# Causal attention: score maxima and chunk sums turned by DMA as 16-bit values, GpSimd's splitting given out in pieces

## What is computed

```python
q = _apply_rope(q, cos, sin)
k = _apply_rope(k, cos, sin)
groups = NH // NKV
k = jnp.repeat(k, groups, axis=2)
v = jnp.repeat(v, groups, axis=2)
scale = HD ** (-0.5)
scores = jnp.einsum('bqhd,bkhd->bhqk', q, k) * scale
causal = jnp.tril(jnp.ones((S, S), dtype=bool))
scores = jnp.where(causal[None, None], scores, jnp.finfo(scores.dtype).min)
probs = jax.nn.softmax(scores, axis=-1)
attn = jnp.einsum('bhqk,bkhd->bqhd', probs, v).reshape(B, S, NH * HD)
```

## Time and profile before

| | us |
|---|---|
| median of 3 runs (1744.45 to 1746.79) | 1745.84 |
| the profiled execution, whole | 1756.45 |
| the profiled execution, span of the trace | 1754.1 |

### The profile page before, as it was taken

How to read it: one execution, slowest core, us unless ns; L and a number is a source line. 1 busy time by engine, 2 the same in 40 slices (tenths; PEclk the granted TensorE clock), 3 DMA queues, 4 the chain that set the end, 5 groups by cost and what they waited for, 6 DMA issues and landing times. The chain is left out here.

```text
span 1754.1 us, 29582 instructions
## 1 busy us (share of the span) xinstructions
PE 1631.0 (93%) x9040; PEld 804.0 (46%) x9040; DVE 1172.6 (67%) x3195; ACT 947.3 (54%) x2069; POOL 553.5 (32%) x842
## 2 busy tenths in 40 slices
PE   7799998899999999999999999998885799999996
PEld 3367655333333333333333333332774355555554
DVE  6632788799888888888888888860765243434342
ACT  6043554166667667676777767767654233333332
POOL 3441338073505003030030300000376244444443
PEclk9899998699999999999999999999986899999999
DMA  5000000321030300303003030000457577777775
GB/s 162 1 7 19 1 2 7 61 42 22 2 61 2 62 2 1 62 2 61 2 2 62 2 61 2 2 1 7 138 193 271 116 130 130 129 130 129 131 125 72
DMA packets 252194, 105.76 MB, mean 60 GB/s; under 512 B 208064, under 2 KB 247880, under 8 KB 252040
## 3 DMA queue, kind: packets, MB, share of 16 engines
q1 hardware_dynamic: 233296, 80.62, 21.6%
q0 software_dynamic: 13392, 18.49, 6.2%
q10 hardware_dynamic: 5352, 4.76, 0.8%
HBM read 30.88 MB, written 23.67 MB: 31 GB/s over the span
## 5 line engine op out<-in xcount | busy, mean ns | idle before, releaser
L1675 ACT ACTIVATE prob<-pS 128x512 f32<-128x512 f32 (+3 forms) x1280 | 597.1, 534 | 256.3 <-PE pS L1563 133.9
L1732 DVE TENSOR_REDUCE mx<-pM 128x1 f32<-128x512 f32 x768 | 503.0, 685 | 70.3 <-PE pM L1543 66.5
L1543 PE MATMUL pM<-KT,QT 96*128 96x512 bf16 (+3 forms) x1280 | 443.6, 356 | 8.7 <-DMA QT<-Qt 4.7
L1559 PE MATMUL pS<-QT,KT 99*128 99x512 bf16 (+3 forms) x1280 | 416.2, 350 | 3.7 <-ACT prob L1675 2.9
L1578 PE MATMUL pO<-prob,VV 128*32 128x512 f32 (+3 forms) x2560 | 299.9, 540 | 14.6 <-ACT prob L1675 14.3
L1728 DVE CUSTOM_DVE_ANT_0 junk<-pM,mask_row 128x128 bf16<-128x128 f32 (+3 forms) x512 | 241.5, 484 | 46.2 <-PE pM L1543 42.9
L2413 PE MATMUL pH<-w13T,QKV 128*128 x568 | 256.8, 595 | 15.4 <-ACT QKV L2439 15.4
L1543 PEld LDWEIGHTS pM<-KT,QT 96*128 96x128 bf16 x1280 | 124.0, 98 | 268.5 <-DVE mx L1732 110.0
L1468 POOL CAST mpart<-mneg 128x16 bf16<-128x16 f32 x32 | 6.8, 211 | 663.2 <-DVE mneg L1740 663.2
L2472 DVE TENSOR_TENSOR QKV<-QKV,pH 128x512 f32<-128x512 f32 x71 | 48.8, 688 | 233.7 <-issue 199.8
L1559 PEld LDWEIGHTS pS<-QT,KT 99*128 99x128 bf16 x1280 | 123.4, 98 | 143.2 <-ACT prob L1675 79.6
(11 more groups left out here) (356 smaller groups left out, 1954.2 us busy)
## 6 DMA issues: line engine op xcount, KB each, us to landing
raw<-in_ffn_w_dram SPq DMA_DIRECT2D x48, 256.0 KB
QKV<-queue SPq DMA_DIRECT2D x71, 136.0 KB, 2.6
out_dram<-x ACTq DMA_DIRECT2D x8, 512.0 KB
x<-_attn_hidden_states_dram SPq DMA_DIRECT2D x14, 256.0 KB, 5.4
QKV<-QKV SPq DMA_TRANSPOSE x142, 2.5
QT<-mrow SPq DMA_DIRECT2D x128, 3.0 KB
out_dram<-QKV POOLq DMA_INDIRECT x71, 3.9
wc_s<-in_attn_Wc_dram SPq DMA_DIRECT2D x1, 1024.0 KB, 8.2
```

The costliest lines, as they stand in the source:

```text
L1543: last = nc.tensor.matmul(pM[:, bank, 0:w], QT[0:ROWS, par, h, qt * P:(qt + 1) * P], KT[0:ROWS, par, 512 * part:512 * part + w], start=Tru ...
L1559: last = nc.tensor.matmul(pS[:, p % NSC, lo:512], KT[0:ROWS + 3, par, kt * P:(kt + 1) * P], QT[0:ROWS + 3, par, h, 512 * c + lo:512 * c + ...
L1675: nc.scalar.activation(prob[:, n % 3, h, lo:512], pS[:, p % NSC, lo:512], ACT.Exp, scale=SCALE).then_inc(s.head_exp, 1)
L1732: nc.vector.reduce_max(mx[:, h, qt, part:part + 1], pM[:, plan.bank[item], 0:w], AX.X).then_inc(s.unit_max, 1)
```

## The change

M leaves PE and ACT. `maxima_parts` writes the parts into columns 0 to 11 of a tile of 4 x 128 columns, the rest of which is zero. SP turns that tile by one DMA transpose (512 columns), waits until it has landed, and then issues the same four DMAs as before (`rows_in`). SP does so in the plan's place of M among its other work.

O leaves PE for every chunk but the last. POOL copies `oS` as 16-bit values, low and high halves apart, into `oh` (`attended_parts`, 1024 values in each partition). SP turns `oh` by one DMA transpose of 1024 columns into `ohT` (`attended_turned`), behind `rows_in` and `turned_in` of that step where there are any. Three steps after that POOL copies the halves together into `oC` (`attended_joined`, 1024 values), and six steps after it DVE divides and stores from `oC` (`chunk_put`). DVE's next `chunk` waits for POOL's copy of the chunk before, not for PE's transposes.

The banks `pM` are handed round among the units alone, and the last O. POOL's queue is now built by step: in each step the maxima's parts, the copies of a chunk's sums, and then at most one piece of other work; `prepare` is cut into six pieces (the keys, and five of the queries). `split` is the same work, in two helpers.

```diff
-        for n, item in enumerate(order):
-            by = {"M": "mrow_out", "U": "unit_max", "O": "o_put"}[item[0]]
+        for n, item in enumerate(x for x in order if x[0] == "U" or x == ("O", CH * NG - 1)):
+            by = {"U": "unit_max", "O": "o_put"}[item[0]]
...
+                def rows_in(k):
+                    par, cols = (k // CH) % 2, slice(512 * (k % CH), 512 * (k % CH) + 512)
+                    sp.wait_ge(s.mparts, k + 1)
+                    if k:
+                        sp.wait_ge(mrow_in[(k - 1) % 2], 64 * ((k - 1) // 2) + 64)
+                    sp.dma_start_transpose(mrow[:, :, :], mpart[:, :, :].rearrange("p j n -> p (j n)")).then_inc(mrow_out[k % 2], 16)
+                    sp.wait_ge(mrow_out[k % 2], 16 * (k // 2) + 16)
+                    for h in range(GRP):
+                        sp.dma_start(QT[ROWS:ROWS + 3, par, h, cols],
+                                     mrow[3 * h:3 * h + 3].rearrange("p j n -> p (j n)")).then_inc(mrow_in[k % 2], 16)
+
+                def attended_turned(k):
+                    sp.wait_ge(s.o_parts, k + 1)
+                    if k:
+                        sp.wait_ge(s.o_join, k)
+                    sp.dma_start_transpose(ohT[:, :, :], oh[:, :]).then_inc(o_in[k % 2], 16)
                 turned_in(0)
-                for k in range(CH * NG):
-                    par, cols = (k // CH) % 2, slice(512 * (k % CH), 512 * (k % CH) + 512)
-                    sp.wait_ge(s.mrow_out, k + 1)
-                    if k >= 2:
-                        sp.wait_ge(mrow_in[k % 2], 64 * (k // 2))
-                    for h in range(GRP):
-                        sp.dma_start(QT[ROWS:ROWS + 3, par, h, cols], mrow[3 * h:3 * h + 3, cols]).then_inc(mrow_in[k % 2], 16)
-                    if k % CH == 2 and k // CH + 1 < NG:
-                        turned_in(k // CH + 1)
+                for x in plan.before:
+                    if x[0] == "M":
+                        rows_in(x[1])
+                for n in range(len(STEPS)):
+                    for x in plan.beside[n]:
+                        if x[0] == "M":
+                            rows_in(x[1])
+                            if x[1] % CH == 2 and x[1] // CH + 1 < NG:
+                                turned_in(x[1] // CH + 1)
+                    for k in contexts(n):
+                        attended_turned(k)
...
+                def attended_parts(k):
+                    pool.wait_ge(s.o_out, k + 1)
+                    if k:
+                        wait_apart(pool, o_in[(k - 1) % 2], 16 * ((k - 1) // 2) + 16)
+                    nc.gpsimd.tensor_copy(oh[:, :].rearrange("p (a n) -> p a n", a=2), apart(oS)).then_inc(s.o_parts, 1)
+
+                def attended_joined(k):
+                    wait_apart(pool, o_in[k % 2], 16 * (k // 2) + 16)
+                    if k:
+                        pool.wait_ge(s.o_put, k)
+                    nc.gpsimd.tensor_copy(apart(oC), ohT[:, :, :].rearrange("p (a j) n -> p a (j n)", a=2)).then_inc(s.o_join, 1)
                 values_in(0)
+                todo = []
+                for n in range(-1, len(STEPS)):
+                    for x in plan.before if n < 0 else plan.beside[n]:
+                        if x in plan.last_unit:
+                            k = plan.last_unit[x]
+                            maxima_parts(k)
+                            first, last = after(k)
+                            todo = first + todo + last
+                    for k in contexts(n):
+                        attended_parts(k)
+                    for k in contexts(n - 3):
+                        attended_joined(k)
+                    if todo:
+                        work(todo.pop(0))
...
-                    for k in contexts(n):
-                        chunk_out(k)
                 values(last_step)
                 chunk_out(CH * NG - 1)
...
                 def chunk(k, n):
                     dve.wait_ge(s.pv, n)
                     if k:
-                        dve.wait_ge(s.o_mm, k)
+                        dve.wait_ge(s.o_parts, k)
                     nc.vector.tensor_copy(oS[:, :], pO[:, :]).then_inc(s.o_out, 1)
...
-                    dve.wait_ge(s.o_mm, k + 1)
-                    o = pM[:, plan.bank[("O", k)], :].rearrange("p (k h d) -> p k h d", k=4, h=GRP)
+                    if k == LAST:
+                        dve.wait_ge(s.o_mm, 1)
+                    else:
+                        dve.wait_ge(s.o_join, k + 1)
+                    o = (pM[:, plan.bank[("O", k)], :] if k == LAST else oC[:, :]).rearrange("p (k h d) -> p k h d", k=4, h=GRP)
...
                 for n, (gi, c, kt) in enumerate(STEPS):
                     for x in plan.beside[n]:
                         beside(x)
-                    for k in contexts(n):
+                    for k in contexts(n - PUT_LATER):
                         chunk_put(k)
                     if n and kt == 0:
                         chunk(CH * gi + c - 1, n)
```

More of the change, by code:

```diff
@@ L1216, in schedule @@
     return before, beside
+LAST = CH * NG - 1
+PUT_LATER = 6
 def contexts(s):
@@ L1248, in __init__ @@
         for k in range(CH * NG):
-            self.units_through[k] = max(self.count[x] for x in order if x[0] == "U" and CH * x[1] + x[3] // 4 == k)
-        self.last_unit = {x: CH * x[1] + x[3] // 4 for x in order
+            self.units_through[k] = max(self.count[x] for x in self.count if x[0] == "U" and CH * x[1] + x[3] // 4 == k)
+        self.last_unit = {x: CH * x[1] + x[3] // 4 for x in self.count
                           if x[0] == "U" and self.count[x] == self.units_through[CH * x[1] + x[3] // 4]}
@@ L1307, in stage6 @@
         f = Names({n: sem("q_" + n) for n in fnames})
+        o_in = [sem(f"c_o_in{n}") for n in range(2)]
+        mrow_out = [sem(f"c_mrow_out{n}") for n in range(2)]
         mrow_in = [sem(f"c_mrow_in{n}") for n in range(2)]
@@ new lines, in after, with work @@
+                def after(k):
+                    gi = k // CH + 1
+                    first = [("keys", gi)] + [("queries", gi, n) for n in range(5)] if k % CH == 1 and gi < NG else []
+                    last = [("norm",)] if k == 2 else []
+                    if k % CH == 3 and gi < NG:
+                        last.append(("values", gi))
+                    return first, last + [("turn", TB + 2 * (k - 1) + n) for n in range(2) if 1 <= k <= TB // 2]
+                def work(item):
+                    if item[0] == "keys":
+                        if item[1] == NKV:
+                            pool.wait_ge(f.turned_pool, NPOOL + TB)
+                        if item[1] == 1:
+                            pool.wait_ge(f.first_ready, 3)
+                        prepare_keys(item[1])
+                    elif item[0] == "queries":
+                        prepare_queries(item[1], item[2])
+                    elif item[0] == "norm":
+                        residual_norm()
+                    elif item[0] == "values":
+                        values_in(item[1])
+                    else:
+                        turn(item[1])
@@ L1494, in _ @@
+                assert not todo
+                for n in range(len(STEPS) - 3, len(STEPS)):
+                    for k in contexts(n):
+                        attended_joined(k)
             @block.tensor
@@ L1664, in _ @@
                         projected_pair(item[1])
-                    else:
-                        beside(item)
                 def exponential(n, h):
@@ L1680, in _ @@
                 for n in range(len(STEPS)):
-                    extra = plan.beside[n]
-                    for place, head in enumerate((0, 1, None, 2, 3)):
-                        for x in extra[place * len(extra) // 5:(place + 1) * len(extra) // 5]:
-                            beside(x)
-                        if n + 1 < len(STEPS) and head is not None:
-                            exponential(n + 1, head)
+                    if n + 1 < len(STEPS):
+                        for h in range(GRP):
+                            exponential(n + 1, h)
             @block.vector
@@ L1770, in _ @@
                         chunk(CH * gi + c - 1, n)
-                chunk(CH * NG - 1, len(STEPS))
-                chunk_put(CH * NG - 1)
+                for n in range(len(STEPS) - PUT_LATER, len(STEPS)):
+                    for k in contexts(n):
+                        chunk_put(k)
+                chunk(LAST, len(STEPS))
+                chunk_put(LAST)
 CAP = B * L + P
```

108 lines of the change are left out of this document (47 added, 61 removed).

## The result

| | before | after |
|---|---|---|
| median, us | 1745.84 (1744.45 to 1746.79) | 1759.62 (1757.58 to 1762.43) |
| ratio, with its 95% interval | | 1.0075 [1.0061, 1.0089] |
| span of the profiled execution, us | 1754.1 | 1760.7 |
| first to last step of the stage, us | 862.3 | 876.9 |

The changed kernel is slower by 13.8 us. The forecast was 5.1 us faster, with a range up to 1757. The last row of the table is the distance from the first value product of the stage to that of its last step, worked out from the trace. The stage alone is 14.6 us longer, which is all of the loss. (The profiled execution of before was itself 10.6 us above its median, so the two spans aren't to be compared.

A forecast was written before the change was run, and what follows sets the result against it. PE was taken to bound the attention's long stretch (420 to 1180 us), DVE's order the chunk ends. Terms: -23.5 - 0.5 + 1.5 + 17.4 = -5.1 us off the 1745.8 median, so 1740.7 us, range 1723 to 1757.

The forecast's parts named there:

- The stall: Place 12, groups 1 to 6: DVE's division waits for late sums, delaying PE's value product; 2.9 us each, 17.4 us lost.
- the prediction's other price: For `turned_in`: at a documented 261 GB/s a wide transpose takes 2.0 us, and DVE waits 0.3 us instead of 2.3.
- Rival 2: POOL's copies of the chunk sums take 2.4 us, so each group loses 5.3 us; 1755.1 us, slower; chance 0.16.
- nothing else is caught: Behind the waiting division at place 12: banks hold four units, PE's own work until the value product is under 2 us.
- fourth rival: Long stretch: PE's freed time doesn't return, as DVE follows too closely; half of 23.5 us lost, 1752.5 us; chance 0.06.
- The saving: PE's stream: 28 Os at 0.43 us and 28 Ms at 0.41 us spared, 23.5 us, plus 0.5 at the start.
- The Ms: Each spares PE 0.41 us: its own 0.32, and the matmul ahead takes 0.22 instead of 0.31; 28 counted.
- the 0.5 for M 1: At the start, M 1 stands between the last early unit and the first scores, DVE idle; 0.5 us saved, an estimate.
- The last chunk: The DMAs of the maxima's rows are issued from 1180.5 instead of 1179.02 us, 1.5 us lost.
- even with no wait: Place 12: the division, formerly at place 5, costs its 0.63 us there even if it needn't wait for the sums.
- Rival 1: At place 12 the sums are back in time, DVE doesn't wait, a group loses 0.63; -18.7, 1727.1 us; chance 0.24.
- Rival 3: DVE's division product from `oC` contends with POOL, 0.6 us more each, 3.6 ahead of the copy; 1744.3 us; chance 0.10.

The follow-up runs named there:

- fill_12: The changed kernel with twelve score products repeated at place 12 of groups 1 to 6, where PE would stand idle: 1753.27 us, ratio 1.0048.
- m_only: The changed kernel with only the maxima turned by DMA; chunk sums go through PE and are divided at once, as before: 1745.74 us, ratio 0.9993.
- sums_first: The changed kernel with SP turning a chunk's sums ahead of the next group's five wide transposes, not behind them: 1736.70 us, ratio 0.9952.
- prepare_whole: The changed kernel with POOL splitting the queries in one go behind the keys, as before, not a piece per step: 1759.52 us, ratio 1.0081.
- put_later_7: The changed kernel with the division seven steps after the turning of the sums instead of six: 1744.08 us, ratio 0.9987.

## Why the prediction was wrong, step by step

**The stall was forecast nearly to the tenth.** The maxima, SP's queue and the copies in the changed kernel, counted from the maxima of each group, against the prediction's chain (its times minus 801.5):

| event | forecast | measured, groups 1 to 6 |
|---|---|---|
| `turned_in` issued to the end | 22.5 | 21.4 to 23.0 |
| sums of c = 0 joined by POOL | 27.3 | 26.4 to 29.2, mean 27.4 |
| value product of place 12 | 31.3 | 30.5 to 33.3, mean 31.5 |

The stall was 17.4 us by forecast and 18.8 measured, from 2.1 to 4.9 us a group where 2.9 was forecast for each. The five wide transposes took 11.9 to 13.4 us, as in the kernel before (12.0 to 13.3), so the 2 us that wide transposes of 2.0 us each would have saved, by the prediction's other price for them, didn't come. Of its terms: the turning of 1024 columns issues in 1.25 us (1.5 forecast), its own landing is 3.2 us in the median, and POOL's copies take 1.04 us to take the halves apart and 1.33 to join them (1.2 for both). Rival 2, with 2.4 us a copy, is out.

```profile
L1403 SPq DMA_TRANSPOSE ohT<-oh x31: 1232/1253/1761, 369.9 to 1203.3; - x31
...
DMA to landing us min/median/max: 3.0/3.2/4.8
```

```profile
L1558 POOL COPY oC<-ohT x31: 1317/1332/1357, 385.1 to 1206.5; 128x1024 uint16<-128x1024 uint16 x31
```

```profile
L1552 POOL COPY oh<-oS x31: 1035/1040/1042, 368.9 to 1202.2; 128x1024 uint16<-128x1024 uint16 x31
```

**The step that failed is what stands behind the stall.** The prediction said of the waiting division that "nothing else is caught", since "the banks hold four units", and counted a stall of 2.9 us as a loss of 2.9. But PE was caught: it ran out of free banks, and its nine waits for DVE's maxima, 15.4 us, are the sign that the prediction had set for its fourth rival. That alone costs nothing more, since the value product waits for the copy in any case: it comes 31.5 us after the maxima, and 31.3 had been forecast. What the prediction left out is how fast PE works afterwards: it looked only for who is late. It read a granted clock of 1.00 in the earlier trace rows and took it as given, though it forecast six gaps of a kind that this stretch didn't have. Measured: +10.9 us at step 12 in six groups, shown by fill_12 to be the clock (9.1 us of it went in the five groups whose clock stayed at full). With this term alone the forecast would have been -5.1 + 10.9 = +5.8 us. The Trainium skill, page "TensorE: Matmul & The Clock Gate", sections "What's actually happening" and "HAM oscillation — how this bites in real kernels", says that TensorE's clock is throttled to half unless the engine's activity releases it, and that waits of TensorE in the middle of a kernel can bring the half clock back each time. The trace agrees (granted 0.50 behind a gap of 2.89 us), though not every wait did it: the one of 2.34 us in the kernel before left the clock at 1.00. It is a rule that spoke against this change, and the prediction hadn't weighed it.

**The saving was 19.8 us and not 24.0.** The price of an O is right: -0.44 at each of the places 0, 4, 12 and 24, 0.43 forecast. But the first group's Os, which the prediction put at nothing, gave it too, so the Os bring 13.6 us and not 12.0. The Ms aren't right: -0.38 at place 19, -0.27 at 23, -0.21 at 30 and 0.00 for the one at place 5. That makes 0.86 us a group where 4 x 0.41 = 1.64 was forecast. The forecast took the M of the earlier trace rows, at 808.22, for all. It is the very one that gives nothing. Four lines further, DVE and then PE in the kernel before:

```profile
808.68 0.68 DVE L1748 COPY oS<-pO 128x512 f32<-128x512 f32 x1
```

```profile
809.47 1.07 PE L1578 MATMUL pO<-prob,VV 128*32 128x512 f32 x8 [0.32 <-ACT prob L1675]
```

This value product opens a chunk and needs the copy of `pO`; it comes 0.79 us after the copy's start, as at 829.98 and 830.76, with PE idle ahead of it. With M gone PE is only idle for longer. m_only agrees: the same three values at 19, 23 and 30, and at this point 2.91 us from one value product to the next, where before had 2.92. So the Ms bring 6.2 us where 12.0 had been counted for them (with the 0.5 for M 1), because all of them were priced by the length of one and not by what ends last behind each. With the 1.6 us more from the Os the saving is 4.2 us short.

**The last chunk: 1.5 forecast, 3.2 measured.** The DMAs of the rows are issued 2.44 us after the transpose's start, as the landing of 2.5 said, and PE's wait is 4.43 where 2.34 + 0.24 stood, so 1.85 us more. For the rest, 1.4 us, no run filled this gap, so the cause is argued: behind it PE is granted 1.2 GHz, where before had 1.00 at this point. The two traces with the last M on PE speak for the clock: behind the same wait (2.79 and 2.78 us) 3.4 and 6.8 us at 1.2 GHz went with a loss of 1.1 and 2.2 us. They also show that the clock falls there without the one wait of 4.43 us.

**The divisions ahead of the copy in groups 0 and 7** cost 1.5 us together. The prediction counted "even with no wait" 0.63 for the groups with a stall only, while the division stands at that place in all eight.

The sum by measured terms: -19.8 + 18.8 + 1.5 + 10.9 + 3.2 = +14.6 us. By forecast: -24.0 + 17.4 + 0 + 0 + 1.5 = -5.1. The difference of 19.7 is 10.9 clock, 4.2 saving, 1.7 last chunk, 1.5 groups 0 and 7, and 1.4 stall.

**The rivals.** None of the four was the case. Rival 1 (sums in time) came true only when SP's order was changed, in sums_first; its -18.7 us would have been 1727, measured 1736.7, since the saving is 4 us smaller, the last chunk 3 us dearer and the divisions of groups 0 and 7 cost 1.5. Rival 3 is a real mechanism, but the changed kernel itself loses nothing by it: its division's product takes up to 0.94 us beside POOL's casts at place 32, and step 32 is at 0.00. Rival 4 failed where it was meant (PE's time comes back at the Os in full) and holds in small for the M at place 5.

What stays open: when a gap is followed by 1.2 GHz, and for how long. Step 12 costs +0.02 us in group 3, with 3.4 us at 1.2 GHz, and +2.15 in groups 2 and 6, with 6.8 us each; the stalls are 2.2, 2.8 and 3.2 us. In prepare_whole groups 1 and 2 have the same stalls as in after with the two lengths exchanged, so the length of the stall alone doesn't set it; no run varied anything else about it. Also open is whether putting the last M back on PE is worth anything.

## What to carry to other kernels

Price a new wait of a busy TensorE twice: by its length, and by what the clock costs behind it, which here was another 58% (10.9 on 18.8 us). A granted clock of 1.00 in the profile before doesn't say what it will be behind a gap that the change brings in. When work is moved onto an in-order queue, look which result on it is wanted soonest and at what its consumer does next: two entries swapped on SP, or a division put two steps later on DVE, turned a loss of 0.75% into gains of 0.5 and 1.0%. And when one price is used for many instances of an instruction, read at least one at each place, since a spared instruction beside a standing wait is worth nothing.

## What the runs showed of the hardware

- In the changed kernel six gaps of 1.45 to 4.23 us in PE's work were each followed by 3.4 or 6.8 us at a granted clock of 0.50 (34.1 us together), and one of 4.43 us in the last chunk by 6.8 us; there eight value products took 1.94 us instead of 1.07. Not every gap was: 2.34 us in the kernel before and 1.34 to 1.48 us in three groups of put_later_7 left it at 1.00. Filling the gap with twelve matmuls whose result is overwritten kept the clock at full speed in five of six groups and made the kernel about 5 to 6 us faster.
- A DMA transpose from SBUF to SBUF of 16-bit values issues in 1.21 us for 512 columns and in 1.25 for 1024, but in 2.50 for 2048 (medians of after; the last from 1.81 to 3.52): between 512 and 1024 columns the issue hardly depends on the size.
- The DVE product of 128x256 from SBUF takes 0.42 us alone, up to 0.94 beside POOL's casts of 1.04 us, and 2.04 beside a POOL subtraction of two SBUF tensors.
- POOL copies 1024 16-bit values per partition in 1.04 us when it reads them strided and in 1.33 when it writes them strided.
